# Moving half of a gate product to slot 29, and four small edits in the router of a Mamba + mixture-of-experts kernel

## What is computed

```
h = layernorm(x) * (1 + ca) + sa
x = x + ga * (h + mamba_forward(norm(h)) + mamba_backward(norm(h)))
h = layernorm(x) * (1 + cb) + sb
x = x + gb * moe(h)
```

## Time and profile before

| | |
|---|---|
| time, median of 3 runs | 2322.68 us (2321.42 to 2323.85) |
| the profiled execution, its own time | 2322.59 us |
| its span in the profile | 2320.8 us |
| VectorE busy | 2184.6 us, 94% of the span |
| GpSimd busy | 2018.6 us, 87% |
| TensorE matmul busy | 1994.2 us, 86% |
| ScalarE busy | 1511.7 us, 65% |

### The profile page before, as it was taken

The page is one execution under the profiler, slowest core; times in us unless marked ns, Lnnn a source line. Parts: engine busy times, 40 slices in busy tenths (PEclk is TensorE's granted clock), DMA queues, the critical chain, the costliest instruction groups (busy, mean ns, idle before and its releaser), DMA issues. The chain is left out here.

```text
span 2320.8 us, 28426 instructions
## 1 busy us (share of the span) xinstructions
PE 1994.2 (86%) x8357; PEld 1121.6 (48%) x8357; DVE 2184.6 (94%) x3338; ACT 1511.7 (65%) x2499; POOL 2018.6 (87%) x1334
## 2 busy tenths in 40 slices
PE   5678988989889898988979899897988989798778
PEld 2444454545545454454544545454554545445443
DVE  5999999999999999999999999999999999999962
ACT  4656666676666767666676666667666676766533
POOL 2778989989898998989899898998989899897955
PEclk8679999999999999999999999999999999999999
DMA  5434444444354444435344443444435344443411
GB/s 156 140 138 141 156 136 144 140 143 151 127 170 133 143 142 142 163 121 167 132 146 140 148 158 130 150 141 143 151 123 174 128 147 142 143 158 119 162 50 42
DMA packets 130703, 323.75 MB, mean 139 GB/s; under 512 B 22260, under 2 KB 46820, under 8 KB 130548
## 3 DMA queue, kind: packets, MB, share of 16 engines
q1 hardware_dynamic: 130548, 321.93, 42.1%
HBM read 315.28 MB, written 6.60 MB: 139 GB/s over the span
## 5 line engine op out<-in xcount | busy, mean ns | idle before, releaser
L517 POOL TENSOR_TENSOR bt<-v,bb 128x1024 f32<-128x1024 f32 x511 | 1208.4, 2368 | 83.3 <-DVE psA L976 69.3
L976 DVE TENSOR_TENSOR_SCAN psA<-psA,bt 128x512 f32<-128x512 f32 x1024 | 1195.7, 1213 | 33.8 <-ACT psA L710 33.1
L710 ACT ACTIVATE psA<-dt,aneg 128x512 f32<-128x512 f32 x1024 | 689.1, 688 | 672.8 <-DVE g L986 671.7
L1232 PEld LDWEIGHTS psY<-ident,g 128*128 128x128 f32 x4096 | 487.8, 146 | 476.3 <-DVE g L986 281.1
L1232 PE MATMUL psY<-ident,g 128*128 128x128 f32 x4096 | 580.8, 284 | 159.0 <-DVE g L986 157.6
L986 DVE TENSOR_TENSOR g<-psA,cb 128x512 f32<-128x512 f32 x1024 | 671.4, 675 | 0.0
L1366 PE MATMUL F<-h2T,w 128*128 128x512 f32 x576 | 327.2, 651 | 119.8 <-DVE pf L1076 117.1
L618 POOL TENSOR_TENSOR act<-pf,gf 128x512 f32<-128x512 f32 x288 | 370.3, 1286 | 53.8 <-DVE pf L1076 43.9
L1403 PE MATMUL F<-act,w 128*128 128x512 f32 x576 | 281.0, 593 | 0.4 <-POOL act L618 0.4
L1248 PE MATMUL psP<-xnT,wcT 128*128 128x512 f32 x496 | 242.9, 613 | 0.1
L1076 DVE SCALAR_TENSOR_TENSOR pf<-tf,F 128x512 f32<-128x512 f32 x288 | 194.5, 675 | 40.9 <-ACT tf L797 37.2
(11 more groups left out here) (185 smaller groups left out, 1846.7 us busy)
## 6 DMA issues: line engine op xcount, KB each, us to landing
bb<-bc_rows SPq DMA_DIRECT2D x256, 512.0 KB, 4.6
cb<-bc_rows SPq DMA_DIRECT2D x256, 512.0 KB, 3.7
wB<-w_rows SPq DMA_DIRECT2D x128, 256.0 KB, 4.8
x<-in_L_attn_x SPq DMA_DIRECT2D x16, 256.0 KB, 4.5
out_x<-osb SPq DMA_DIRECT2D x16, 256.0 KB, 4.4
modA<-mod_table SPq DMA_DIRECT2D x15, 192.0 KB, 4.7
w<-in_L_ffn_ew SPq DMA_DIRECT2D x2, 1024.0 KB, 7.6
bc_rows<-xd SPq DMA_DIRECT2D x32, 64.0 KB, 3.0
```

What stands on the lines that cost most here:

```text
L517: g.tensor_tensor(bt[:, n % 2, :, :], v[d][:, :, :], bb[:, n // 2 % 2, n % 2, :].unsqueeze(1).broadcast_to([P, NH, T]), ALU.mult).then_inc ...
L710: s.activation(psA[:, half * T:half * T + T], dt_[d][:, half, :], ACT.Exp, scale=aneg[d][:, half, n:n + 1]).then_inc(a_s, 1)
L976: w.tensor_tensor_scan(ah, ah, bt[:, n % 2, half, :][:, order], 0.0, ALU.mult, ALU.add)\
L1232: last = m.matmul(psY[:, half * T + i * P:half * T + i * P + P], g_[:, n % 2, half, i * P:i * P + P], ident[:, :], is_transpose=True, star ...
```

## The change

- The second half of direction 0's gate product moves: TensorE's turn from slot 18 to slot 28, VectorE's product from slot 18 to slot 29, the last thing in that slot. The order of psP's pieces follows.
- `DOWN_SLOTS`: four down projections come earlier (20 to 18, 21 to 20, 24 to 21, 28 to 24), so that slot 28 has two in place of three.
- Router: the difference `gd` is computed by GpSimd from `top` in SBUF, at the start of its slot 8 work, and ScalarE's exponential waits for it (`gd_s`). The copy `topv` and the cast `topf` are gone. `iota8` is uint32, and the two comparisons take `iota8` and `topi`, both uint32 in SBUF.
- The stores of zero in `statistics` are gone.

```diff
-POST_F_SLOT = 17
+POST_F_SLOTS = (17, 28)
+GATE_F_SLOTS = (17, 29)
...
-DOWN_SLOTS = [10, 11, 15, 16, 17, 18, 20, 21, 24, 28, 28, 28, 29, 29, 29, 30, 30, 31]
+DOWN_SLOTS = [10, 11, 15, 16, 17, 18, 18, 20, 21, 24, 28, 28, 29, 29, 29, 30, 30, 31]
...
-def piece(d, kind, half=0):
-
-    return 1 + PREP * d + kind + half
+def piece(b, d, kind, half=0):
+
+    return PIECES * b + (1 + PREP if d else 1 if b == 0 else 0) + kind + half
...
-    no_xn = 1 if isinstance(b, int) and b == NB - 1 else 0
-    return PIECES * b + PIECES - 1 + half - no_xn
+    if b == NB - 1:
+        return PIECES * NB - NH + half
+    return PIECES * (b + 1) + (PREP if half else -1)
...
-        iota8 = sb("iota8", [P, NX])
+        iota8 = sb("iota8", [P, NX], u32)
...
                 if slot == GATE_SLOT + 1:
+                    pool.wait_ge(gate_s, GATES * fb + NT)
+                    g.tensor_tensor(gd[:, :], top[:, :, 1], top[:, :, 0], ALU.subtract).then_inc(gd_s, 1)
                     pool.wait_ge(ge_s, fb + 1)
                     g.tensor_tensor(gs[:, :], ge[:, :], ones[:, :], ALU.add).then_inc(gw_s, 1)
...
-                        act_e.wait_ge(gate_s, GATES * (b - 1) + GATE_D)
+                        act_e.wait_ge(gd_s, b)
                         s.activation(ge[:, :], gd[:, :], ACT.Exp).then_inc(ge_s, 1)
...
-                w.memset(stat_[:, :, 4], 0.0)
...
                 q = GATES * fb
-                topf = F2[:, 2 * NT * NX:2 * NT * NX + 2 * NT].rearrange("p (k c) -> p k c", c=2)
-                topv = F2[:, 4 * NT * NX:4 * NT * NX + NT]
                 dve.wait_ge(F2_full, FULLS * fb + GATE + 1)
+                wait(dve, ge_s, fb)
                 for i in range(NT):
                     w.max(top[:, i, :], F2[:, i * NX:(i + 1) * NX]).then_inc(gate_s, 1)
-                dve.wait_ge(gate_s, q + 4)
-                w.tensor_copy(topv, top[:, :, 1]).then_inc(gate_s, 1)
+                dve.wait_ge(gate_s, q + NT)
                 for i in range(NT):
                     w.max_index(topi[:, i, :], top[:, i, :], F2[:, i * NX:(i + 1) * NX]).then_inc(gate_s, 1)
-                dve.wait_ge(gate_s, q + 5)
-                wait(dve, ge_s, fb)
-                w.tensor_tensor(gd[:, :], topv, top[:, :, 0], ALU.subtract).then_inc(gate_s, 1)
-                dve.wait_ge(gate_s, q + 9)
-                w.tensor_copy(topf, topi[:, :, 0:2]).then_inc(gate_s, 1)
-                dve.wait_ge(gate_s, q + 11)
+                dve.wait_ge(gate_s, q + 2 * NT)
                 wait(dve, wts_s, 3 * fb)
                 for j in range(2):
                     w.tensor_tensor(hot[:, j, :, :], iota8[:, :].unsqueeze(1).broadcast_to([P, NT, NX]),
-                                    topf[:, :, j:j + 1].broadcast_to([P, NT, NX]), ALU.is_equal)\
+                                    topi[:, :, j:j + 1].broadcast_to([P, NT, NX]), ALU.is_equal)\
                         .then_inc(F2_free if j else gate_s, 1)
...
-                    if scan_ and slot - POST_F_SLOT in (0, 1):
-                        gate_y(b, 0, slot - POST_F_SLOT)
+                    if scan_ and slot in GATE_F_SLOTS:
+                        gate_y(b, 0, GATE_F_SLOTS.index(slot))
```

More of the change, by code:

```diff
@@ L61 @@
 FOLD_SLOT, FINAL_SLOT, COPY_SLOT, OUT_SLOT = 0, 1, 2, 3
-def piece(d, kind, half=0):
-    return 1 + PREP * d + kind + half
+def piece(b, d, kind, half=0):
+    return PIECES * b + (1 + PREP if d else 1 if b == 0 else 0) + kind + half
 def xn_piece(b):
-    return 0 if isinstance(b, int) and b == 0 else PIECES * b - NH
+    return PIECES * b - NH if b else 0
 def post_piece(b, half):
-    no_xn = 1 if isinstance(b, int) and b == NB - 1 else 0
-    return PIECES * b + PIECES - 1 + half - no_xn
+    if b == NB - 1:
+        return PIECES * NB - NH + half
+    return PIECES * (b + 1) + (PREP if half else -1)
 def up_at(slot):
@@ L399, in rows_out @@
             def rows_out(b, d):
-                sp.wait_ge(pP_free, PIECES * b + piece(d, XD) + 1)
+                sp.wait_ge(pP_free, piece(b, d, XD) + 1)
                 sp.dma_start(bc_dram[d], xd[R:R + 2 * N, :]).then_inc(brow_out, 16)
@@ L559, in make_dt @@
             def make_dt(b, d):
-                pool.wait_ge(pP_free, PIECES * b + piece(d, DT, 1) + 1)
+                pool.wait_ge(pP_free, piece(b, d, DT, 1) + 1)
                 pool.wait_ge(sp_s, 5 * (2 * b + d) + 5)
@@ L718, in keep_y, with take @@
                     s.activation(yg[d][:, half, :], psY[:, half * T:half * T + T], ACT.Copy).then_inc(acc_s, 1)
-            def take(b, pos):
-                act_e.wait_ge(pP_full, PIECES * b + pos + 1)
+            def take(pos):
+                act_e.wait_ge(pP_full, pos + 1)
             def silu(b, d, half):
-                take(b, piece(d, U, half))
+                take(piece(b, d, U, half))
                 s.activation(psP[:, :], psP[:, :], ACT.Identity, scale=0.5,
@@ L740, in prep @@
                 if k == XD_AT:
-                    take(b, piece(d, XD))
+                    take(piece(b, d, XD))
                     wait(act_e, brow_out, 16 * (2 * b + d))
@@ L747, in prep @@
                     q = 5 * (2 * b + d)
-                    take(b, piece(d, DT, half))
+                    take(piece(b, d, DT, half))
                     wait(act_e, dt_s, 2 * b + d)
@@ L828, in first_u @@
             def first_u(bank, half):
-                act_e.wait_ge(pP_full, piece(0, U, half) + 1)
+                act_e.wait_ge(pP_full, piece(0, 0, U, half) + 1)
                 s.activation(bank, bank, ACT.Identity, scale=0.5, bias=convb[0][:, half:half + 1]).then_inc(xh_s, 1)
@@ L835, in first_dt @@
             def first_dt(bank, half):
-                act_e.wait_ge(pP_full, piece(0, DT, half) + 1)
+                act_e.wait_ge(pP_full, piece(0, 0, DT, half) + 1)
                 s.activation(ab[:, half, :], bank, ACT.Abs, bias=bdt[0][:, half:half + 1]).then_inc(sp_s, 1)
@@ L867, in _ @@
             first_u(F1[:, :], 1)
-            act_e.wait_ge(pP_full, piece(0, XD) + 1)
+            act_e.wait_ge(pP_full, piece(0, 0, XD) + 1)
             s.activation(xd[:, :], psA[0:R + 2 * N, 0:T], ACT.Copy).then_inc(pP_free, 1)
@@ L1161, in _ @@
             dve.wait_ge(sp_s, 5)
-            dve.wait_ge(pP_free, piece(0, DT, 1) + 1)
+            dve.wait_ge(pP_free, piece(0, 0, DT, 1) + 1)
             w.tensor_tensor(dt_[0][:, :, :], xb[:, :, :], ab[:, :, :], ALU.add).then_inc(dt_s, 1)
@@ L1239, in open_piece @@
                 def open_piece(kind, half=0):
-                    wait(pe, pP_free, PIECES * b + piece(d, kind, half))
+                    wait(pe, pP_free, piece(b, d, kind, half))
                 if k - U_AT in (0, 1, 3, 4):
@@ L1305, in side @@
             def side(b, slot, prep_b, prep_f, post_f):
-                if post_f and slot in (POST_F_SLOT, POST_F_SLOT + 1):
-                    half = slot - POST_F_SLOT
+                if post_f and slot in SKIP_SLOTS:
+                    skip(0, SKIP_SLOTS.index(slot))
+                if post_f and slot in POST_F_SLOTS:
+                    half = POST_F_SLOTS.index(slot)
                     pe.wait_ge(acc_s, 4 * b + 2)
@@ L1310, in side @@
                     turn(psP, 0, half, False).then_inc(pP_full, 1)
-                if post_f and slot in SKIP_SLOTS:
-                    skip(0, SKIP_SLOTS.index(slot))
                 if prep_f is not None:
@@ L1338, in ffn_side @@
                     pe.wait_ge(wts_s, 3 * fb + 3)
-                    pe.wait_ge(pP_free, min(PIECES * (fb + 1) + piece(1, DT, 1) + 1, PIECES * NB))
+                    pe.wait_ge(pP_free, min(piece(fb + 1, 1, DT, 1) + 1, PIECES * NB))
                     for i in range(NT):
@@ L1421, in _ @@
             first_u(F1[:, :], 1)
-            pe.wait_ge(pP_free, piece(0, XD))
+            pe.wait_ge(pP_free, piece(0, 0, XD))
             for half in range(NH):
@@ L1426, in _ @@
             last.then_inc(pP_full, 1)
-            pe.wait_ge(pP_free, piece(0, DT))
+            pe.wait_ge(pP_free, piece(0, 0, DT))
             m.matmul(psA[:, T:2 * T], wdtT[0][:, 0, :], xd[0:R, :], start=True, stop=True).then_inc(pP_full, 1)
```

6 lines of the change are left out of this document (3 added, 3 removed).

## The result

Ten runs of each kernel: before 2323.26 us, after **2328.67 us** (median; 2325.67 to 2332.48). The ratio is 1.0024, with a 95% interval of 1.0015 to 1.0032: slower by 0.15 to 0.32%. One run of before, 3683.79 us, was disturbed and is left out of the ratio. The forecast was 2326.4 us, inside a range of 2309 to 2330. By the forecast's own classes 2328.67 is slower (above 2327.3), to which it gave 0.28, and not within 0.2% of before, to which it gave 0.42.

What follows compares the result with a forecast made beforehand. VectorE's instruction queue was taken to bound each pass. Router +13.2 us, moved product -8.4 and zero stores -1.0 gave +3.8 on the profiled 2322.6 us, so 2326.4 us, range 2309 to 2330.

Steps and rivals of the forecast that it cites:

- The bound: All scanning passes: a pass lasts as long as VectorE's instructions, plus a few short waits for ScalarE; GpSimd is ahead.
- The comparisons wait for the end of GpSimd's product: Slot 7: router comparisons, both inputs in SBUF, are held until L517 ends; 15 x 1.00 = 15.0 us lost.
- The delayed four-element sum of the setup: Setup: GpSimd sum beside L945 took 0.48 us against a 0.205 us median; taken as evidence for a wait.
- L951 beside the power: Setup: VectorE's two-SBUF-input L951 kept its plain 0.48 us for two beside GpSimd's 1.29 us power; evidence for no wait.
- Slot 9's give-back: Slot 9, six passes: the 0.35 us wait for ScalarE's tanh shrinks to 0.05; 6 x 0.30 = 1.8 us back.
- The copy, subtraction and cast, 0.28 us without a wait: Slot 7: with these gone from VectorE, the comparisons are ready 0.28 us earlier a pass, if nothing holds them.
- The moved product: Slot 18 loses 0.60 us; slot 29 hides it in the 0.57 us wait before slot 30's scan; 8.4 us gained.
- The zero stores: Removing 62 ns stores: those in slots 10 and 29 give nothing, slot 4's gives 16 x 0.06 = 1.0 us.
- No wait: Rival, slot 7: the comparisons are not held, 11.9 us gained, 2310.7 us; chance 0.30.
- The second comparison held too: Rival, slot 7: GpSimd's subtraction slips between the comparisons, 0.20 us more a pass, +3.0, 2329.4 us; chance 0.15.
- Slot 29 failing: Rival: slot 29 does not hide the product, up to 0.60 us a pass returns, 2334.8 or 2319.1 us; chance 0.04.
- The sum: Whole kernel: +13.2 router, -8.4 moved product, -1.0 zero stores = +3.8 us, giving 2326.4 us.

Runs made afterwards that it cites:

- e2: The kernel after, with the index searches writing their unsigned indices into PSUM, so the comparisons have one SBUF input, without a cast; 2313.16 us, ratio 0.9957.
- e8: The kernel after, with its two comparisons issued in slot 8 between scan and expert product, where GpSimd waits for VectorE; 2307.26 us, ratio 0.9930.
- e7: The kernel after with indices in PSUM, plus an unused four-element two-input SBUF product in slot 5 beside GpSimd's power; 2311.38 us in one run.
- e9: The kernel after with indices in PSUM, plus an unused four-element two-input SBUF product in slot 7 beside GpSimd's products; 2331.09 us in one run.
- e5: The kernel before, with the cast writing its float copy of the indices to SBUF in place of PSUM; 2338.74 us, ratio 1.0072.
- e11: The kernel after with indices in PSUM, plus an unused four-element float copy, SBUF to SBUF, in slot 7 beside GpSimd's products; 2325.04 us in one run.
- e10: The kernel after with indices in PSUM, plus an unused four-element reciprocal, SBUF to SBUF, in slot 7 beside GpSimd's products; 2310.90 us in one run.
- e3: The kernel before with only the moved half product, its piece numbers and the new order of down projections; 2313.72 us, ratio 0.9958.
- e6: The kernel after with indices in PSUM, and slot 29's product computed twice, once into an unread buffer; 2319.16 us, ratio 0.9984.
- e1: The kernel after with the cast of the indices to float in PSUM put back and iota8 in float again; 2314.28 us, ratio 0.9959.

## Why the prediction was right, step by step

- **The bound** held. VectorE's queue sets the time; no engine took over, and both halves of the change moved the end by what they did to that queue.
- **The comparisons wait for the end of GpSimd's product**: the step on which the forecast turned, and shown. It had 1.00 us a pass; slot 7 grew by 1.005, from passes with 0.80 (pass 1) to 1.96 us (pass 11) for the pair, and the ends stand 0.20 us behind GpSimd's product each time. e2 takes the stall away by the operand's place alone, e8 by the time alone. The term counted 15 passes: 15 x 1.005 = 15.1.
- **Why it read the row rightly, and what it did not know.** The delayed four-element sum of the setup pointed the right way, though there the GpSimd sum, recorded as starting 0.01 us ahead, was the one drawn out: that row shows a conflict and not who yields. L951 beside the power was no exception but another case: e7 shows 0.150 us beside the power, e9 a median of 1.48 beside the products, with one and the same instruction. That the product holds because it streams from SBUF all the while, and the power does not because it then only computes, is the reading that fits both; it was not tested by itself. The prediction's condition, two inputs in SBUF, was too narrow: a copy or a cast with one is held as well (e5, e11). And "no VectorE instruction of the passes has two inputs in SBUF" overlooked L1085, which reads `wB` and one column of `modC` there beside `F2` in PSUM. In the kernel before it keeps its length beside GpSimd's streaming products (in pass 7 it runs from 1064.54 to 1065.28 us, inside GpSimd's 128 x 512 product of 1064.32 to 1065.60), so a one-column operand did not make it wait. Its 32, all of them beside such products, have one length:

```profile
L1085 DVE SCALAR_TENSOR_TENSOR apart<-F,modC,wB x32: 737/739/751, 236.8 to 2278.9; 128x512 f32<-128x512 f32 x32
```

The Trainium skill, "SBUF — State Buffer", section "Who interferes with whom", has both: two SBUF inputs contend with a GpSimd instruction that reads SBUF, and copies and casts can enter modes in which they use the port pair shared with GpSimd, while the second to come blocks fully. e5, e9 and e11 agree with it, and so does e10's reciprocal, which is not in its list; "for the whole instruction", as it says, e7 does not bear out beside the power.
- **Slot 9's give-back**: 1.8 us predicted; slot 9 gave 14 x 0.085 = 1.2 and slot 10 another 0.4. The reverse, that an earlier router only lengthens the wait there, is seen in e2 (4.383 against 4.264 us).
- **The copy, subtraction and cast, 0.28 us without a wait**: 0.255 in e2.
- **The moved product**: 14 x 0.60 = 8.4 us predicted, 14 x 0.598 = 8.4 in slot 18, and slot 29 unchanged. The margin there was 0.01 us (what is left of the hole in front of the scan) and not 0.57 less 0.54, since the store that was to give 0.06 gave nothing; e3, which keeps the stores, has slot 29 at 5.286 all the same. By itself it is worth 7.65, since slot 13 returns 0.6 to an expert's wait. That the room in slot 29 is as small as said is shown by e6: predicted 0.57 us for a second product, measured 0.51 in passes 1 to 13.
- **The zero stores**: the term that was mis-sized. 16 x 0.06 = 1.0 us was predicted and slot 4 lost 0.004 us a pass, under 0.1 us in all. The timeline of slot 4 of the kernel before shows why:

```profile
1020.17 0.87 DVE L992 BATCH_NORM_STATS2 stF<-x 128x6 f32<-128x128 f32 x4
1021.09 0.17 DVE L996 BATCH_NORM_AGGREGATE statF<-stF 128x2 f32<-128x6 f32 x1
1021.12 0.06 DVE L994 MEMSET statF<- 128x4 f32 x1
1021.18 0.28 DVE L996 BATCH_NORM_AGGREGATE statF<-stF 128x2 f32<-128x6 f32 x3
```

The store stands inside the first aggregate's time, where the aggregate has only to wait for the four statistics. In the kernel after the four aggregates take 0.38 us from 0.04 behind the statistics, as they did before (1021.09 to 1021.46). The row of its duration was right; it was not asked whether the next instruction could have started without it.
- **The rivals.** No wait: refuted by every run with the two operands in SBUF there. The second comparison held too, behind GpSimd's subtraction: in pass 7 the subtraction (1038.21 to 1038.40) and the second comparison (which ends at 1038.44) ran side by side, the subtraction at its plain 0.19 us and the comparison at 0.23, and slot 7's 1.005 us has no room for the 0.20. Slot 29 failing: refuted. Its figures for "taking pass 1's or pass 4's wait for all passes", 2319 and 2337 us, add the waits of 0.56 and 1.70 us where the delays against before, 0.28 and 1.42, belong; by its own terms they are 2315.6 and 2332.7. Neither the sum nor the chances use them.
- **The sum**: +3.8 us was predicted for all passes, +3.8 is what passes 1 to 14 show in the profiled executions, and +3.6 what everything behind the first scan shows. That is closer than the terms are, and so partly luck. For passes 1 to 14 alone the prediction's terms give 14.0 - 1.5 - 8.4 - 0.9 = +3.2 us; measured were +14.1 in slot 7, -1.6 in slots 9 and 10, -8.4 in slot 18, -0.1 in slot 4 and -0.2 in the others. For the rest they give +0.6, and measured was -0.15 (passes 0 and 15 +0.5, the tail -0.6). The two errors cancel in the whole. The forecast of 2326.4 is 2.3 us below the measured 2328.67. The profiled execution has just that much in its setup, a term that the prediction did not have; the others' setups are not on record.
- **What stays open** is that setup. The first scan stood between 44.99 us (e11) and 49.42 (e1) in the profiled executions of all kernels, whose setup has the same matmuls, and it goes with the granted clock of the 45 us ahead of it (before 0.77 and 1.00 in the two windows shown, after 0.66 and 0.89, e1 0.66 and 0.66). The setup's program is not the cause by itself: e2 has that of the kernel after, and its first scan stood at 45.81 us, with 0.77 and 1.00. The mean granted clock of the ten runs of after was 0.947 to 0.954, that of twenty-five runs of before 0.953 to 0.958; in the profiled executions the share of the clock that was not granted, added up over the span, comes to 97.6 us before and 110.0 after. Of these 12.4 us more, 8.1 lie in passes 1 to 14, where VectorE sets the time, and 5.1 in the first 45 us, ahead of the first scan. How often each kernel's runs meet the lower clock in the setup is not shown, and no experiment was made on it.

## What to carry to other kernels

A small VectorE instruction whose operands all lie in SBUF, if it has two inputs or is a copy or a cast, can cost ten times its length when GpSimd is streaming (the reciprocal did not). Put one of two inputs, or a cast's result, in PSUM, or issue it where GpSimd waits, and do not judge by the length that it had with PSUM in it. When an edit bundle comes out near zero, run its halves alone: here +12.4 and -7.7 us lay behind +3.8, and keeping the good half and mending the bad one gave 0.7% over the kernel before. Work may be put into a wait up to the wait's own length, and before removing an instruction "for its duration" look whether the next one could start without it.

## What the runs showed of the hardware

- A VectorE copy of 128 x 4 floats from SBUF to SBUF took a median of 1450 ns and up to 2054 beside GpSimd's 128 x 1024 product, a two-input product of the same size 1481 ns; a reciprocal of that size 158 ns, a two-input product beside GpSimd's power 150 ns, and a cast of 128 x 8 with its result in PSUM 170 ns against 1241 in the mean with it in SBUF.
- A VectorE instruction with a full and a one-column input in SBUF and a third in PSUM (L1085, 128 x 512) was not held beside GpSimd's products: 737 to 751 ns in all 32.
- A stall of this kind is shown as busy time: VectorE's rose by 14.9 us (2184.6 to 2199.5) while its waits fell.
- A store of zeros of 62 ns ran inside the time of a neighbouring aggregate and was worth nothing.
- An instruction that waits for the result just written costs some 0.12 us more than the same instruction with other work between (e2 against e8).
